# Attention on one core: values and ones stand in the array in two column groups, the probabilities move, and VectorE divides straight into the transposed layout

## What is computed

```python
qkv = layernorm(x) @ w_qkv.T + b_qkv            # 16 heads of 16 channels
q, k = apply_rope(q, sin, cos), apply_rope(k, sin, cos)
att = einsum('bhtd,bhsd->bhts', q, k) / 4
att = where(causal, -inf, att)
att_prob = softmax(att, axis=-1)
att_v = einsum('bhts,bhsd->bhtd', att_prob, v)
x = x + att_v.reshape(B, T, C) @ w_out.T + b_out
```

## Time and profile before

| | us |
|---|---|
| median of 3 runs | 3294.53 (3293.99 to 3295.24) |
| the profiled execution | 3290.8 |
| its span, first instruction to last | 3288.9 |
| TensorE busy | 2928.9 (89%) |
| VectorE busy | 2503.2 (76%) |
| ScalarE busy | 2093.2 (64%) |
| GpSimd busy | 1808.7 (55%) |

### The profile page before, as it was taken

One profiled execution on the slowest core, in us unless ns is written; L12 is line 12 of the kernel. 1 busy time (PEld: TensorE's weight loads), 2 busy tenths in 40 slices (PEclk: granted clock), 3 DMA queues, 4 the chain that ended last, 5 costly groups with the idle time before them and its releaser, 6 DMA issues.

```text
span 3288.9 us, 60848 instructions
## 1 busy us (share of the span) xinstructions
PE 2928.9 (89%) x19888; PEld 2424.0 (74%) x19888; DVE 2503.2 (76%) x6373; ACT 2093.2 (64%) x4556; POOL 1808.7 (55%) x1913
## 2 busy tenths in 40 slices
PE   4999999945669999999999999999999999987863
PEld 3777777734558888888888888888888888865652
DVE  4556665574668788788888888888888888889986
ACT  2555655523447777777777777777777777754531
POOL 1111111132677667676676767768676686766442
PEclk9999999957889999999999999999999999989985
DMA  2000000002575656746656566566666566543311
GB/s 94 1 0 0 0 0 0 1 26 74 162 201 165 194 181 176 208 142 200 199 165 197 159 195 194 163 195 177 181 188 184 174 176 196 162 131 91 102 34 51
DMA packets 572119, 422.72 MB, mean 129 GB/s; under 512 B 228691, under 2 KB 475219, under 8 KB 571734
## 3 DMA queue, kind: packets, MB, share of 16 engines
q1 hardware_dynamic: 571862, 419.51, 44.0%
HBM read 276.39 MB, written 143.01 MB: 128 GB/s over the span
## 4 chain that ended last, share of the span: by engine, by line
PE 73%; DVE 12%; POOL 7%; ACT 3%; issue 3%; DMA 1%; SPq 0%; DVEq 0%; POOLq 0%; ACTq 0%
PE bank L1987 25%; PE bank L2038 15%; PE bank L2135 6%; PE bank L1841 5%; POOL oT L805 4%; PE bank L2043 3%; PE bank L1753 3%; PE bank L1816 3%; PE bank L1826 3%; PE bank L2018 2%; PE bank L2026 1%; ACT oT L1092 1%; DVE acc L1534 1%; PE bank L1795 1%; PE bank L1811 1%
## 5 line engine op out<-in xcount | busy, mean ns | idle before, releaser
L772 POOL TENSOR_TENSOR acc<-acc,shifted 128x510 f32<-128x510 f32 x384 | 585.6, 1527 | 553.7 <-DVE acc L1534 550.5
L1534 DVE SCALAR_TENSOR_TENSOR acc<-bank,conv_w,acc 128x254 f32<-128x254 f32 (+1 forms) x1536 | 628.6, 471 | 98.5 <-ACT acc L1022 95.1
L1987 PE MATMUL bank<-x_k,w_kq 128*128 128x256 f32 x2048 | 503.6, 391 | 13.0 <-DMA x_k<-xT_scratch 8.9
L1020 ACT ACTIVATE shifted<-bank,conv_w 128x255 f32<-128x255 f32 x768 | 367.0, 478 | 217.9 <-issue 147.3
L1022 ACT ACTIVATE acc<-bank,conv_b,conv_w 128x256 f32<-128x256 f32 x768 | 439.9, 573 | 0.0
L1987 PEld LDWEIGHTS bank<-x_k,w_kq 128*128 128x128 f32 x2048 | 378.4, 194 | 80.8 <-issue 31.8
L789 POOL TENSOR_TENSOR inv<-inv,outer 128x30 f32<-128x30 f32 (+14 forms) x480 | 258.4, 538 | 37.6
L2135 PE MATMUL bank<-w_o,oT 128*128 128x256 f32 x1024 | 246.3, 385 | 33.5 <-POOL oT L805 33.5
L786 POOL TENSOR_TENSOR outer<-inv 128x30 f32<-128x30 f32 (+14 forms) x480 | 236.2, 492 | 30.6 <-DMA inv<-L_scratch 2.8
L1987 PE MATMUL bank<-x_g,w_g 128*128 128x256 f32 x1024 | 251.1, 389 | 0.0
L2018 PE MATMUL bank<-kq 128*128 128x256 f32 x1024 | 244.4, 382 | 5.1 <-ACT kq L1032 4.0
(11 more groups left out here) (235 smaller groups left out, 6539.9 us busy)
## 6 DMA issues: line engine op xcount, KB each, us to landing
abc<-decay_scratch SPq DMA_DIRECT2D x64, 512.0 KB, 6.0
q_scratch<-kq SPq DMA_DIRECT2D x64, 512.0 KB, 6.9
L_scratch<-LM SPq DMA_DIRECT2D x64, 512.0 KB, 3.5
M_scratch<-LM SPq DMA_DIRECT2D x64, 512.0 KB, 6.7
LTm<-L_scratch SPq DMA_DIRECT2D x64, 512.0 KB, 4.5
MTm<-M_scratch SPq DMA_DIRECT2D x128, 256.0 KB, 4.3
kqm<-q_scratch SPq DMA_DIRECT2D x64, 512.0 KB, 4.1
k_scratch<-knw SPq DMA_DIRECT2D x64, 258.0 KB, 4.8
```

Of the source, the lines that this page charges most:

```text
L772: pool.tensor_tensor(dst, dst, shifted[:, u % 2, :, 1:], ALU.add).then_inc(Z["sumk" if u < 4 else "sumv"], 1)
L1020: act.activation(shifted[:, u % 2, i % 2, 1:], pj[:, 0:SEQ - 1], ACT.Copy, scale=conv_w[:, kind, bass.ds(head, 1), TAPS - 2:TAPS - 1].rear ...
L1534: dve.scalar_tensor_tensor(out=acc[:, kind, i, t:], in0=pj[:, 0:SEQ - t], scalar=wcol, in1=acc[:, kind, i, t:], op0=ALU.mult, op1=ALU.add) ...
L1987: mm = pe.matmul(dst[:, i * SEQ:(i + 1) * SEQ], w[:, k, head * DK:(head + 1) * DK], x[:, k, :], start=(k == 0), stop=(k == CT - 1))
```

## The change

The standing operand of the weighted values is now vx, 64 columns a head: the 16 values at column 0 or 16 (by r, the parity of the head in its half), sixteen ones at column 32 or 48, zeros elsewhere. The moving operand is probT, 128 columns. The heads of an even unit write partitions 0 to 63 of the bank and those of an odd unit 64 to 127, interleaved instruction by instruction; `apply` takes a pair of units and waits for both copies. Heads that share a bank region add into it, since the other's columns are zero. The result is channels x tokens already: for each head 16 rows of sums and, 32 partitions further, 16 equal rows of the probabilities' sum. VectorE takes the reciprocal of the whole bank (128 x 512) and multiplies quarter by quarter (32 partitions, 256 elements each) into attT. The transposes of att, their copy and the two semaphores between are gone; `project_att` waits for VectorE. In the body, `apply(pair - 4)` now stands between weigh(pair - 2) and weigh(pair - 1).

```diff
...
         xT = sa("xT", [P, CT, SEQ])
         rope_t = sa("rope_t", [P, 4, TPS, 2 * HEADS * HALF])
         rot = sa("rot", [P, TPS, 2 * HEADS, SLOT])
-        vx = sa("vx", [P, TPS, HEADS, HD + 1])
+        vx = sa("vx", [P, TPS, HEADS, 4 * HD])
         qT = sa("qT", [P, 2, 4, SEQ])
         q_scale = sa("q_scale", [P, 2])
         kT = sa("kT", [P, 4, SEQ])
         row_min = sa("row_min", [P, 4, 4])
         prob = sa("prob", [P, 4, 512])
         probT = sa("probT", [P, 4, 512])
-        rsum = sa("rsum", [P, TPS, HEADS])
-        att = sa("att", [P, TPS, C])
+        rsum = sa("rsum", [P, 4 * P])
         attT = sa("attT", [P, CT, SEQ])
         stack_a.close()
         stack_f0.close()
...
             for i in range(4):
                 pool.memset(q_scale[i * SLOT:(i + 1) * SLOT, i % 2:i % 2 + 1], -float(HD) ** -0.5).then_inc(consts, 1)
             pool.wait_ge(consts, 12)
-            pool.memset(vx[:], 1.0).then_inc(consts, 1)
+            zeroed = pool.memset(vx[:], 0.0)
+            ch.link(zeroed)
+            for r in range(2):
+                ins = pool.memset(vx[:].rearrange("p j (a r) d -> p (j a) r d", r=2)[:, :, r, (2 + r) * HD:(3 + r) * HD], 1.0)
+            ins.then_inc(consts, 1)
             pool.wait_ge(loaded_bias, 32)
             ch.link(pool.tensor_copy(bias_part[:, 0], bias[:]))
             ch.link(pool.tensor_tensor(bias_rest[:], bias[:], bias_part[:, 0], ALU.subtract))
...
                 act.wait_ge(A["qkv"], past(3 * b + 3))
                 act.wait_ge(A["av"], past(UNITS * b))
                 for j in range(TPS):
-                    act.copy(vx[:, j, :, 0:HD], bank[4][:, j * C:(j + 1) * C].rearrange("p (h d) -> p h d", d=HD)).then_inc(A["v"], 1)
+                    d = vx[:, j]
+                    values = bass.AP(tensor=d.tensor, offset=d.offset, ap=[list(d.ap[0]), [8 * HD, HEADS // 2], [5 * HD, 2], [1, HD]])
+                    act.copy(values, bank[4][:, j * C:(j + 1) * C].rearrange("p (a r d) -> p a r d", r=2, d=HD)).then_inc(A["v"], 1)
 
             def turned_in(b, j):
 
...
             def signs(T, g, w):
                 act.wait_ge(R["xf"], past(g + 1))
                 act.activation(T["sgn"][:, 0:w], T["xf"][:, 0:w], ACT.Sign).then_inc(R["sign"], 1)
-
-            def att_turned(b):
-                act.wait_ge(A["attTp"], past(b + 1))
-                act.copy(attT[:].rearrange("p k t -> p (k t)"), bank[3][:]).then_inc(A["attT"], 1)
 
             def body(b, more):
 
...
                         act.wait_ge(A["av"], past(UNITS * b + u - 3))
                     act.copy(probT[:, u % 4], bank[6 + u % 2][:]).then_inc(A["probT"], 1)
 
-                if not first(b):
-                    att_turned(b - 1)
                 exps(0), exps(1)
                 turned(0), exps(2), turned(1), exps(3)
                 for pair in range(4, UNITS, 2):
...
 
                 def weighted_values(j):
                     dve.wait_ge(A["av"], past(UNITS * b + (UNITS if j else 4)))
-                    av = bank[(3, 1)[j]][:, 0:HEADS * (HD + 1)].rearrange("p (h d) -> p h d", d=HD + 1)
-                    c.link(dve.reciprocal(rsum[:, j, :], av[:, :, HD]))
-                    dve.tensor_tensor(att[:, j].rearrange("p (h d) -> p h d", d=HD), av[:, :, 0:HD],
-                                      rsum[:, j, :].unsqueeze(2).broadcast_to([P, HEADS, HD]), ALU.mult).then_inc(A["att"], 1)
+                    c.link(dve.reciprocal(rsum[:], bank[(3, 1)[j]][:]))
+                    for q in range(4):
+                        rows, half = 2 * P // 4 * (q % 2), P // 4
+                        av = bank[(3, 1)[j]][:].rearrange("p (k m t) -> p k m t", k=CT, m=2)[:, :, q // 2]
+                        ins = dve.tensor_tensor(attT[q * half:(q + 1) * half, :, j * P:(j + 1) * P], av[rows:rows + half],
+                                                rsum[:].rearrange("p (k m t) -> p k m t", k=CT, m=2)[rows + half:rows + 2 * half, :, q // 2], ALU.mult)
+                    ins.then_inc(A["att"], 1)
 
                 minima(0), minima(1)
                 if not first(b):
...
                                           rot[:, j, h0:h0 + 4, :].rearrange("p h d -> p (h d)"), ident[:])
                     mm.then_inc(A["rotp"], 1)
 
-            def att_turned(b):
+            def project_att(b):
                 pe.wait_ge(A["att"], past(2 * b + 2))
-                for k in range(CT):
-                    for j in range(TPS):
-                        mm = pe.transpose(bank[3][:, k * SEQ + j * P:k * SEQ + (j + 1) * P], att[:, j, k * P:(k + 1) * P], ident[:])
-                mm.then_inc(A["attTp"], 1)
-
-            def project_att(b):
-                pe.wait_ge(A["attT"], past(b + 1))
                 for j in range(TPS):
                     dst = bank[1][:, j * C:(j + 1) * C]
                     pe.matmul(dst, ones3[:], bias_rows[:, 3 * C:], start=True, stop=False)
...
                     mm.then_inc(A["pT"], 1)
 
                 def apply(u):
-                    hs, j = unit(u)
-                    pe.wait_ge(A["probT"], past(UNITS * b + u + 1))
+
+                    j = unit(u)[1]
+                    pe.wait_ge(A["probT"], past(UNITS * b + u + 2))
                     if u == 0:
                         pe.wait_ge(A["v"], past(2 * b + 2))
-                        if not first(b):
-                            pe.wait_ge(A["attT"], past(b))
                     if u == 4:
                         pe.wait_ge(A["res"], past(b))
-                    for m, (g, r, half) in enumerate(hs):
-                        h = 4 * g + 2 * half + r
+                    pairs = list(zip(unit(u)[0], unit(u + 1)[0]))
+                    for m, pair in enumerate(pairs):
                         for st in range(j + 1):
-                            mm = pe.matmul(bank[(3, 1)[j]][:, h * (HD + 1):(h + 1) * (HD + 1)],
-                                           probT[:, u % 4, (m * (j + 1) + st) * P:(m * (j + 1) + st + 1) * P], vx[:, st, h, :],
-                                           start=(st == 0), stop=(st == j))
-                    mm.then_inc(A["av"], 1)
+                            for e, (g, r, half) in enumerate(pair):
+                                mm = pe.matmul(bank[(3, 1)[j]][half * P // 2:(half + 1) * P // 2, g * P:(g + 1) * P], vx[:, st, 4 * g + 2 * half + r, :],
+                                               probT[:, (u + e) % 4, (m * (j + 1) + st) * P:(m * (j + 1) + st + 1) * P],
+                                               start=(u in (0, 4) and m == 0 and st == 0), stop=True, skip_group_check=True)
+                                if m == len(pairs) - 1 and st == j:
+                                    mm.then_inc(A["av"], 1)
 
                 scores(0)
                 if not first(b):
-                    att_turned(b - 1), project_att(b - 1)
+                    project_att(b - 1)
                 scores(2), weigh(0), weigh(1)
                 for pair in range(4, UNITS, 2):
-                    scores(pair), apply(pair - 4), weigh(pair - 2), apply(pair - 3), weigh(pair - 1)
+                    scores(pair), weigh(pair - 2), apply(pair - 4), weigh(pair - 1)
                     if pair == 8 and more:
                         tokens(b + 1)
                 if more:
                     queries_keys(b + 1, 0)
-                apply(8), weigh(10)
+                weigh(10), apply(8)
                 if more:
                     queries_keys(b + 1, 1)
-                apply(9), weigh(11)
+                weigh(11)
                 if more:
                     values_in(b + 1)
-                apply(10), apply(11)
+                apply(10)
                 if more:
                     rotated(b + 1, 0), rotated(b + 1, 1)
 
...
                 tokens(0), queries_keys(0, 0), queries_keys(0, 1), values_in(0), rotated(0, 0), rotated(0, 1)
 
             sequences(pe, start, body)
-            att_turned(SEQS - 1), project_att(SEQS - 1)
+            project_att(SEQS - 1)
 
             def select(turn):
                 T = tiles[turn]
```

More of the change, by code:

```diff
@@ L354, in program @@
             "xn", "xTp", "xT", "qkv", "rope", "v", "rotp", "qkT", "score", "low", "exp", "pT",
-            "probT", "av", "att", "attTp", "attT", "yout", "res", "var", "rstd")}
+            "probT", "av", "att", "yout", "res", "var", "rstd")}
         R = {k: sem("R_" + k) for k in (
@@ L933, in _ @@
             sequences(act, start, body)
-            att_turned(SEQS - 1)
             def select(turn):
```

## The result

The changed kernel takes 3338.12 us, the median of four runs (3336.06 to 3343.14), beside 3294.89 for the kernel before: ratio 1.0136, 95% interval 1.0124 to 1.0148, or +43.2 us. The profiled execution is the longest of the four, 3343.14 us (span 3341.3), 52.3 us above the profiled one of before.

What follows compares the result with a forecast made beforehand. TensorE bounds the kernel before; afterwards a ring through three engines adds 1.40 us a sequence. Fourteen steps +19.6, sequence 0 +3.2, last sequence +5.8 sum to +28.6 on 3294.53: 3323 us, 8 in 10 within 3303 to 3356.

Steps and rivals of the forecast that it cites:

- The ring: Attention sequence, projection to projection: TensorE, VectorE and ScalarE wait for each other in turn; 39.20 us against 37.80, +1.40.
- 1, projection to minima 6: TensorE from the output projection through scores 6 until VectorE's minima, with one call of 1.2 us: 9.98 us.
- 3, division 0: VectorE's first division of a sequence, between minima 7 and 8: reciprocal 3.5 us plus four products, 4.88 us.
- 7, to the projection: VectorE's second division, behind rope and the router's last part, until the output projection starts: 5.03 us.
- its own range: Whole kernel: 3306 to 3342 us, from reciprocals of 3.2 to 3.65, calls of 1.0 to 1.4 and some clock falls; 69%.
- the rival with a fall in each of the two gaps: TensorE gaps ahead of projection and tokens' transposes: a fall to 1.2 GHz after each, 28 times 1.7 us, +48, 3371; 7%.
- a granted clock of the stage clearly below 0.99: Attention stage in the profile after: seeing this would show the forecast wrong.
- The ends: Sequence 0 and the last sequence, outside the fourteen steps: +3.2 and +5.8 us.
- the streaming rival: The two divisions: reciprocal of 0.69 us hides behind TensorE, 34.2 us a sequence, about -51, 3244 us; 5%.
- eight plain steps: VectorE's reciprocal: eight steps an element, 4.4 us each, +29 more, 3352 us; 10%.
- The column halves: TensorE's weighted values: rival that they don't overlap, calls of 2.0 us, +37 more, 3360 us; 3%.
- The case of 1.2 us a call and 3.5 us a reciprocal: TensorE's calls and VectorE's reciprocals in attention: the forecast itself, +28.6, 3323 us; 69%.

Runs made afterwards that it cites:

- filled: Changed kernel plus nine unused bf16 products of 128x512 on TensorE ahead of the output projection and of the tokens' transposes; 3317.2 us, ratio 1.0067.
- the run with two copies: Both reciprocals of the changed kernel become plain copies of the same bank, so the division is left out; 3231.28 us, ratio 0.9802.
- the first with both divisions in halves: Changed kernel with each division in two halves of 256 columns, tile 1's upper half in bank 3, tokens' transposes later; 3281.23 us, ratio 0.996.
- the last kernel: Against the 3281.23 us kernel with halved divisions: tile 1's heads reordered by groups, tokens' transposes later, call 8 waits for bank 3; 3259.81 us, ratio 0.9897.

## Why the prediction was right, and where a term was off

**The ring, leg by leg.** In the changed kernel's step from 346.98 to 387.93, by the rows above; "filled" is the kernel with filled gaps, from 333.83 to 373.15, whose VectorE starts minima 6 at 343.85, the reciprocals at 346.57 and 367.98, minima 8 at 351.70 and rope at 363.17:

| leg | forecast | changed | filled |
|---|---|---|---|
| 1, projection to minima 6 | 9.98 | 11.64 | 10.02 |
| 2, to division 0 | 2.72 | 2.72 | 2.72 |
| 3, division 0 | 4.88 | 5.13 | 5.13 |
| 4 and 5, to rope | 11.78 | 11.48 | 11.47 |
| 6, to division 1 | 4.81 | 4.82 | 4.81 |
| 7, to the projection | 5.03 | 5.16 | 5.17 |
| sum | 39.20 | 40.95 | 39.32 |

Leg by leg the ring is the one that was forecast, at full clock 0.12 us longer, and the runs with one reciprocal left out show both divisions on it. The reciprocal takes 3.35 us for a forecast of 3.5. Its four products take 1.71 instead of 1.36: they follow each other every 0.43 us, not 0.34. A call takes 1.03 for the 1.2 that was taken; the transposes ahead of it take 0.59 for the 0.47 (355.04 to 355.63), which no run explains. The gaps, 2.46 and 2.32, were worked out as 2.2; ScalarE's wait of some 5 us is 5.32.

**The term that was mis-sized is the clock.** The forecast let only some falls into its own range and gave the rival with a fall in each of the two gaps 7%, at 28 falls of 1.7 us. The price held behind the projection's gap (leg 1 is 1.62 us longer) and not behind the tokens' (0.3, the first step), where TensorE waits at call 6 anyway. The number lies between the two cases: 11 of 14 steps have a fall behind the projection, four behind the tokens. Filling the gaps took 21 us off the median, half of the 43. The argument against the rival was that the fall of the earlier trace rows came after no idle time, which is true and says nothing on whether gaps bring on falls. And the forecast had named a granted clock of the stage clearly below 0.99 as a sign that it is wrong: from the first projection to the last the clock is 0.94, where it was 0.99 before. By that sign its account of the clock failed, though the time lies in its range.

**The ends.** The forecast gave +3.2 and +5.8; the changed kernel has +6.0 and +10.0. With filled gaps they are +5.4 (97.96 for 92.58) and +6.6 (34.94 for 28.30). So of the last sequence's excess 3.4 us are clock. In sequence 0, TensorE stands still for 6.04 us ahead of the tokens, and the groups behind that run at half clock (the call at 80.89 takes 1.94 us); in the filled kernel the wait there is still 4.10 us, and the call behind it takes 1.60.

**The sum.** With filled gaps the last projection starts 683.29 - 653.47 = 29.8 us later than before, close to the forecast's +28.6. That it is so close is partly luck: the 14 steps give +17.8 for a forecast of +19.6, since the two half-clock places of before have no like with filled gaps, and the ends give +12.0 for +9.0. The clock adds 28.3 in the profiled execution (24.3 in the 14 steps, 4.0 at the ends), which makes the 58.1. The median of +43.2 is smaller, since the profiled execution is the longest of the four. Then 5.8 come back, in a stage that the forecast had left at nothing. There, in the kernel before, a group of 64 products ran at half clock; the groups of before and of the changed kernel, behind the attention stage:

```profile
L1898 PE MATMUL bank<-table,ohT 64*128 64x131 f32 x64 | 16.5, 439 | 0.6 <-ACT ohT L941 0.6
```

```profile
L1893 PE MATMUL bank<-table,ohT 64*128 64x131 f32 x64 | 9.0, 283 | 0.8 <-DVE table L1401 0.8
```

VectorE's longest wait there, for a ScalarE step behind them, is 6.9 us where it was 12.1. It isn't an effect of this change as such: in the run with two copies and in the first with both divisions in halves the 60 us behind the stage have a granted clock of 0.52 as before, in the changed, the filled and the last kernel 0.61 to 0.64. What decides it is open.

**The other rivals.** The reciprocal doesn't stream (3354 ns for 512 elements against 688 for the copy). With copies in its place the step is 34.13, as the streaming rival's 34.2 had it. It isn't eight plain steps either: (3354 - 254) / 496 = 6.25 ns an element, six of the 1.04 ns steps. The Trainium skill (VectorE: DVE Perf Modes, First, the fixed hardware budget) names a repeat count of 8; read as cycles an element it doesn't agree with this trace, which has six. The column halves overlap in part: 1.51/1.03 = 1.47. The Trainium skill (TensorEngine Tiling (Array Packing), Theoretical Speedup) has up to 2x for 64 columns, and the runs stay within that. The case of 1.2 us a call and 3.5 us a reciprocal held because its errors were small and of both signs: the calls' legs -0.3, the divisions' +0.25 and +0.13.

## What to carry to other kernels

An operation moved to an engine with free time costs its latency, not its busy time, once the engines wait for each other in a ring: here the 3.7 us a sequence that the new products can save were worth nothing until the long divisions were cut in halves and set between steps that others wait for. When a forecast opens idle gaps on TensorE, price the clock behind each gap as a term of the sum, by what follows the gap: 1.6 us where the ring ran on at half clock, 0.3 where TensorE had a wait ahead of it anyway. Test it early with filler products. Compare steps with the same falls in the same place: steps of different clocks hide here that the two divisions cost the same.

## What the runs showed of the hardware that was not expected

- A gap of 2.46 us on TensorE was followed by some 3 us at 1.2 GHz in 11 of 14 steps of the changed kernel and in 14 of 14 without tile 0's reciprocal; nine bf16 products in the gap (2.12 us) kept the clock at 2.4 GHz. A gap of 2.32 us ahead of the tokens was followed by a fall in four of 14 steps of the changed kernel, and in nine of 14 without tile 1's reciprocal; the order of work on TensorE is the same in all of them. What decides is open.
- Two column halves in turns take 1.03 us for 16 instructions, one half after the other 1.51: a factor of 1.47. Instructions with 64 standing columns, not interleaved, still take 1.51/16 = 0.094 us, less than the 0.11 of the whole array.
- The reciprocal takes 3354 ns for 512 elements a partition and 1752 for 256, from a bank, and 3349 from SBUF in the kernel before.
- Products on 32 partitions take 418 ns for 256 elements, as those on 128 do (0.42 us), but the four of a division, which lie on different partitions, follow each other every 0.43 us instead of 0.34.
